# Query and key projections and scores of the last context attention from rounded high parts and remainders

## The reference

```python
x = x + _L3_xattn_ref(_layernorm(x, axis=-1), ctx_1024, ctx_1024, ...)

B, S, D = (1, 1024, 256)
H, DK, DV = (16, 64, 64)
q = (queries @ Wq.T + bq).reshape(b, sq, H, DK).transpose(0, 2, 1, 3)
k = (keys @ Wk.T + bk).reshape(b, sk, H, DK).transpose(0, 2, 1, 3)
v = (values @ Wv.T + bv).reshape(b, sk, H, DV).transpose(0, 2, 1, 3)
scores = jnp.einsum('bhqd,bhkd->bhqk', q, k) / jnp.sqrt(jnp.float32(DK))
causal = jnp.triu(jnp.ones((sq, sk), bool), k=1)
scores = jnp.where(causal, jnp.float32(-jnp.inf), scores)
attn = jax.nn.softmax(scores, axis=-1)
out = jnp.einsum('bhqk,bhkd->bhqd', attn, v)
out = out.transpose(0, 2, 1, 3).reshape(b, sq, H * DV)
return out @ Wo.T + bo
```

## Time and profile before

| | |
|---|---|
| median of three executions | 1660.79 us |
| span of the profiled execution | 1661.7 us |
| TensorE busy | 1562.1 us, 94% of the span |
| VectorE, ScalarE, GpSimd busy | 66%, 55%, 28% |
| share of TensorE in the chain that ended last | 72% |
| TensorE busy in 1380 to 1570 us, in the stage `l3_xattn` | 189.2 of 190 us |
| VectorE, ScalarE, GpSimd busy there | 109.3, 104.4, 59.7 us |
| mean granted clock of TensorE | 0.987 |

### The profile page before, as it was taken

One profiled execution on the slowest core, in us unless ns is written; L12 is line 12 of the kernel. 1 busy time (PEld: TensorE's weight loads), 2 busy tenths in 40 slices (PEclk: granted clock), 3 DMA queues, 4 the chain that ended last, 5 costly groups with the idle time before them and its releaser, 6 DMA issues.

```text
span 1661.7 us, 22981 instructions
## 1 busy us (share of the span) xinstructions
PE 1562.1 (94%) x7755; PEld 844.1 (51%) x7755; DVE 1089.4 (66%) x2220; ACT 908.5 (55%) x1750; POOL 466.0 (28%) x565
## 2 busy tenths in 40 slices
PE   8999999989998999999979999999988989999998
PEld 3476454448784444444335555555344445545446
DVE  7764054775547799999658888887367526555515
ACT  5432233534336677778557777877325635555613
POOL 0220100120000555555205655656020103323300
PEclk9999999999999999999999999999998999999999
DMA  6001000010010000000254311110166020000000
GB/s 244 1 1 27 19 0 1 38 76 1 26 31 15 10 20 10 11 10 30 82 184 147 105 30 30 44 44 21 45 161 166 25 83 24 13 22 12 1 1 26
DMA packets 37707, 76.25 MB, mean 46 GB/s; under 512 B 4507, under 2 KB 23451, under 8 KB 36155
## 3 DMA queue, kind: packets, MB, share of 16 engines
q1 hardware_dynamic: 37590, 74.78, 14.0%
HBM read 57.89 MB, written 16.78 MB: 45 GB/s over the span
## 4 chain that ended last, share of the span: by engine, by line
PE 72%; DVE 12%; issue 7%; ACT 6%; SPq 1%; POOL 1%; PEldq 1%; DMA 1%; PEld 0%; DVEq 0%; POOLq 0%; ACTq 0%
PE ps L2499 6%; PE ps L2081 3%; PE ps L3418 3%; PE ps L2057 3%; PE ps L2103 3%; PE ps L2488 3%; PE ps L3383 3%; PE ps L3393 3%; PE ps L3438 2%; PE ps L230 2%; PE ps L2510 2%; PE ps L2067 2%; PE ps L3411 2%; PE ps L3451 2%; PE ps L857 2%
## 5 line engine op out<-in xcount | busy, mean ns | idle before, releaser
L2754 POOL TENSOR_TENSOR work<-work,arena_b 128x512 f32<-128x512 f32 x128 | 168.4, 1318 | 115.9 <-ACT work L2618 115.9
L2708 DVE CUSTOM_DVE_ANT_0 work<-ps,arena_a 128x1024 f32<-128x1024 f32 x128 | 154.6, 1209 | 0.4 <-PE ps L2488 0.4
L2600 ACT ACTIVATE work<-work,small 128x1024 f32<-128x1024 f32 x128 | 146.8, 1147 | 4.3 <-DVE small L2708 4.3
L2499 PE MATMUL ps<-identity,work 128*128 128x128 f32 x1024 | 139.0, 277 | 6.0 <-ACT work L2618 1.8
L2499 PEld LDWEIGHTS ps<-identity,work 128*128 128x128 f32 x1024 | 115.1, 142 | 54.6 <-issue 29.4
L3600 POOL TENSOR_SCALAR ctx_keys<-ctx_keys,small 128x128 f32<-128x128 f32 (+3 forms) x128 | 66.9, 535 | 173.3 <-DVE small L3525 173.3
L2720 DVE TENSOR_TENSOR work<-ps,arena_b 128x512 f32<-128x512 f32 x128 | 87.9, 686 | 32.9 <-PE ps L2499 30.8
L2618 ACT ACTIVATE work<-ps 128x512 f32<-128x512 f32 x128 | 76.3, 596 | 57.9 <-PE ps L2499 55.0
L2273 POOL TENSOR_SCALAR work<-work 128x1024 f32<-128x1024 int32 x64 | 66.6, 1040 | 100.7 <-DVE work L2228 100.3
L2488 PE MATMUL ps<-work 96*128 96x512 bf16 x256 | 79.3, 393 | 13.5 <-DVE small L2708 7.7
L3477 ACT ACTIVATE ctx_keys<-ctx_keys,small 128x128 f32<-128x128 f32 (+3 forms) x128 | 70.7, 553 | 28.6 <-DVE small L3517 28.0
(11 more groups left out here) (454 smaller groups left out, 3532.8 us busy)
## 6 DMA issues: line engine op xcount, KB each, us to landing
work<-parts_k_L_xattn SPq DMA_DIRECT2D x14, 384.0 KB, 3.9
arena_a<-in_mask SPq DMA_DIRECT2D x2, 2048.0 KB, 7.5
arena_b<-in_groupT SPq DMA_DIRECT2D x2, 2048.0 KB, 9.7
head_weights<-in_w_L_xattn SPq DMA_DIRECT2D x8, 449.0 KB, 3.3
arena_a<-in_w_l_attn SPq DMA_DIRECT2D x1, 3072.0 KB, 16.1
head_weights<-in_w_L_attn SPq DMA_DIRECT2D x8, 384.0 KB, 3.1
work<-parts_q_L_attn SPq DMA_DIRECT2D x8, 384.0 KB, 4.5
work<-parts_k_L_attn SPq DMA_DIRECT2D x8, 384.0 KB, 5.2
```

The lines of the kernel that those rows point to most:

```text
L2499: mm = pe.transpose(t_psum[z][:, kt * P:(kt + 1) * P], prob[i % NP][:, o:o + P], k.iden[:, :])
L2600: act.activation(p, p, ACT.Exp, scale=-1.0, bias=minmax[:, i % 8:i % 8 + 1], accum_out=sums[:, i % 8:i % 8 + 1]).then_inc(*exped.up())
L2708: dve.tensor_tensor_reduce(prob[i % NP], s_psum[i % NS], NEG[:, b, qt, :], -1.0, BIG * 3e8, OP.add, OP.min, minmax[:, i % 8:i % 8 + 1]).th ...
L2754: pool.tensor_tensor(p, p, GT[:, b, 4:8, qt * P:(qt + 1) * P], OP.mult).then_inc(*weighed_pool.up())
```

## The change

Queries, keys and their inputs are each held as a rounded high part and the exact remainder, and each product of two such numbers becomes three: high by high, high by low, low by high. The lowest product is left out.

- Normalisation: VectorE writes the rounded high part of each block, then the full one as before, then the remainder (`Norm.scale`), for both halves.
- Context: GpSimd splits it once, in the stage before; weights: GpSimd splits those of each group, two groups ahead, at the end of the group before (`CausalParts`).
- Chunks of q and k: six matmuls for two. ScalarE reads the bank first and writes the rounded high part, with bias; VectorE reads it again and writes the remainder, and only then is the bank free. The chunks of v stay as they are.
- Scores: six matmuls for two. The factor 0.125 moves into the maximum instruction.
- q and k of one batch of a group lie in rings of three buffers of 512 columns, for two of 1024.
- The weight rounding of the following stage uses one scratch piece for four.

```diff
     def scale(self, dve, n):
         k, dst = self.k, self.dst[n]
         dve.wait_ge(*self.rooted(n + 1))
+        if self.high:
+            for c in range(DC):
+                dve.tensor_tensor(self.high[n][c], dst[:, c, :], self.tmp[n], OP.mult).then_inc(*self.topped.up())
         for c in range(DC):
             final = dst[:, c, :] if self.put is None else self.put[n][:, c, :]
             if self.w is None:
@@ -252,6 +265,12 @@
             dve.wait_ge(*self.scaled(2 * n + c + 1))
             op = dve.tensor_scalar(final, dst[:, c, :], k.col(self.w, c), k.col(self.b, c), OP.mult, OP.add)
         op.then_inc(*self.out.up())
+        if self.high:
+            dve.wait_ge(*self.topped(2 * n + 2))
+            dve.wait_ge(*self.out(n + 1))
+            for c in range(DC):
+                dve.tensor_tensor(self.low[n][c], dst[:, c, :], self.high[n][c].bitcast(F32),
+                                  OP.subtract).then_inc(*self.rest.up())
...
+        if nxt:
+            causal_parts.split_context(pool)
...
+        if nxt:
+            causal_parts.split_weights(pool, 0, k.ahead["l3_xattn"][0](1))
...
+    def split_context(self, pool):
+        for n in range(B):
+            for c in range(DC):
+                pool.tensor_scalar(self.ctx_high[n][c], self.raw[n][c], 1.0, 0.0, OP.mult, OP.add).then_inc(*self.ctx_top.up())
+        for x in range(B * DC - 1):
+            self.split_low(pool, x)
+
+    def split_low(self, pool, x):
+        n, c = divmod(x, DC)
+        pool.wait_ge(*self.ctx_top(x + 1))
+        pool.tensor_tensor(self.ctx_low[n][c], self.raw[n][c], self.ctx_high[n][c].bitcast(F32),
+                           OP.subtract).then_inc(*self.ctx_rest.up())
+
+    def split_weights(self, pool, g, loaded):
+        pool.wait_ge(*loaded)
+        for j in range(2):
+            pool.tensor_scalar(self.w_high[g % 2][j], self.w_raw[g % 2][j], 1.0, 0.0, OP.mult, OP.add).then_inc(*self.w_top.up())
+        for j in range(2):
+            pool.wait_ge(*self.w_top(2 * g + j + 1))
+            pool.tensor_tensor(self.w_low[g % 2][j], self.w_raw[g % 2][j], self.w_high[g % 2][j].bitcast(F32),
+                               OP.subtract).then_inc(*self.w_rest.up())
...
-    q = [view(w, s * K, NT) for s in range(2)]
-    kT = [view(w, (2 + s) * K, NT) for s in range(2)]
+    parts = k.ahead["causal_parts"]
+    blocks = k.rounded("causal_qk", "work", 0, 4 * K)
+    q_high, k_high, q_low = ([view(blocks, (3 * o + j) * S, S) for j in range(min(3, 8 - 3 * o))] for o in range(3))
+    unused = [k.rounded(f"causal_qk_{c}{n}", "ctx_feat", c * NT * 2 + n * S2 + S, S)[:, :] for c in range(DC) for n in range(B)]
+    q_low, k_low = [*q_low, unused[0]], unused[1:]
+    qk_high, qk_low = dict(q=q_high, k=k_high), dict(q=q_low, k=k_low)
...
+    QK = [x for x, ch in enumerate(CHUNKS) if ch[1] != "v"]
+    place = {CHUNKS[x][:3]: y + 1 for y, x in enumerate(QK)}
+    made = lambda g, n: max(place[g, "q", n], place[g, "k", n])
...
-    chunk_out = lambda x: {"q": q_out, "k": k_out, "v": v_out}[CHUNKS[x][1]](2 * CHUNKS[x][0] + CHUNKS[x][2] + 1)
+    chunk_out = lambda x: (v_out(2 * CHUNKS[x][0] + CHUNKS[x][2] + 1) if CHUNKS[x][1] == "v" else rest(place[CHUNKS[x][:3]]))
...
-                n, q0 = n_keys(i), b * S + qt * P
+                n = n_keys(i)
+                j = (2 * g + b) % 3
                 if i % nk == 0:
-                    pe.wait_ge(*q_out(2 * g + b + 1))
-                    pe.wait_ge(*k_out(2 * g + b + 1))
+                    pe.wait_ge(*rest(made(g, b)))
                 if i >= 2:
                     pe.wait_ge(*maxed(2 * i - 2))
-                for h in range(nh):
-                    r = slice(h * rows, (h + 1) * rows)
-                    mm = pe.matmul(s_bank[i % 2][:, h, 0:n], q[g % 2][r, q0:q0 + P], kT[g % 2][r, b * S:b * S + n],
-                                   start=True, stop=True)
+                for qs, ks in ((q_high, k_high), (q_high, k_low), (q_low, k_high)):
+                    for h in range(nh):
+                        r = slice(h * rows, (h + 1) * rows)
+                        mm = pe.matmul(s_bank[i % 2][:, h, 0:n], qs[j][r, qt * P:(qt + 1) * P], ks[j][r, 0:n],
+                                       start=ks is k_high and qs is q_high, stop=qs is q_low)
...
-                    src, t0 = (k.Hn, n * S) if what == "q" else (k.ctxT, n * S2)
+                    high, low = (parts.x_high, parts.x_low) if what == "q" else (parts.ctx_high, parts.ctx_low)
+                    w_high, w_low = (ws[g % 2][what == "k"] for ws in (parts.w_high, parts.w_low))
+                    pe.wait_ge(*parts.w_rest(2 * g + 2))
                     for c in range(DC):
-                        if g == 0 and what == "q":
-                            pe.wait_ge(*ln.rows(n, c))
-                        mm = pe.matmul(ps, W[g % 2][what == "k"][:, c, :], src[:, c, t0:t0 + S], start=c == 0,
-                                       stop=c == 1)
+                        if g == 0:
+                            pe.wait_ge(*(ln.topped if what == "q" else parts.ctx_top)(2 * n + c + 1))
+                        pe.matmul(ps, w_high[:, c, :], high[n][c], start=c == 0, stop=False)
+                        pe.matmul(ps, w_low[:, c, :], high[n][c], start=False, stop=False)
+                    for c in range(DC):
+                        if g == 0:
+                            pe.wait_ge(*(ln.rest if what == "q" else parts.ctx_rest)(2 * n + c + 1))
+                        mm = pe.matmul(ps, w_high[:, c, :], low[n][c], start=False, stop=c == 1)
...
-                if what == "k":
+                if what != "v":
+                    y = 2 * g + n
                     act.wait_ge(*part(x + 1))
-                    if g >= 2:
-                        act.wait_ge(*scored(per * (g - 1)))
-                    act.activation(kT[g % 2][:, half(n)], chunk_bank(x), ACT.Identity,
-                                   bias=weights[g % 2][:, 897:898]).then_inc(*k_out.up())
+                    if y >= 3:
+                        act.wait_ge(*scored(nk * (y - 2)))
+                    act.activation(qk_high[what][y % 3], chunk_bank(x), ACT.Identity,
+                                   bias=weights[g % 2][:, 896 + (what == "k"):897 + (what == "k")]).then_inc(*top.up())
...
-                    dve.tensor_tensor_reduce(prob[i % NP][:, h, 0:n], s_bank[i % 2][:, h, 0:n], causal[:, S - n:S], -1.0,
+                    dve.tensor_tensor_reduce(prob[i % NP][:, h, 0:n], s_bank[i % 2][:, h, 0:n], causal[:, S - n:S], -0.125,
...
-                if what == "q":
-                    dve.wait_ge(*part(x + 1))
-                    if g >= 2:
-                        dve.wait_ge(*scored(per * (g - 1)))
-                    dve.tensor_scalar(q[s][:, half(n)], chunk_bank(x), weights[s][:, 896:897], 0.125, OP.add,
-                                      OP.mult).then_inc(*q_out.up())
+                if what != "v":
+                    y = (2 * g + n) % 3
+                    dve.wait_ge(*top(place[g, what, n]))
+                    dve.scalar_tensor_tensor(out=qk_low[what][y], in0=chunk_bank(x),
+                                             scalar=weights[s][:, 896 + (what == "k"):897 + (what == "k")],
+                                             in1=qk_high[what][y].bitcast(F32), op0=OP.add, op1=OP.subtract).then_inc(*rest.up())
...
+        parts.split_low(pool, B * DC - 1)
+        pool.wait_ge(*ln.var_done(2))
+        parts.split_weights(pool, 1, w_in[1](1))
...
+            if step % per == per - 1 and step // per + 2 < G:
+                g = step // per + 2
+                parts.split_weights(pool, g, w_in[g % 2](g // 2 + 1))
```

44 lines of the change are left out of this document (37 added, 7 removed).

## The result

| | before | changed |
|---|---|---|
| median, us | 1660.68 (1659.28 to 1661.01, 4 executions) | 1680.54 (1677.61 to 1686.22, 4 executions) |
| ratio | | 1.0118, 95% interval 1.0103 to 1.0133 |
| profiled execution: time, span | span 1661.7 | 1681.16, span 1679.9 |

The change makes the kernel 1.2% slower; 1674 was forecast, in a range of 1661 to 1685.

The account below looks back on a forecast made before the run. TensorE was taken as the bound in the stage's groups. Start 4.8, groups 1 to 6 5.1, last group -0.4 and clock 3.5 gave +13.0 us on the 1660.8 median: 1674 us, own range 1668 to 1680, wider 1661 to 1685.

Parts of the forecast that it names:

- TensorE's saving, 1.82 per group: TensorE in each group: q and k chunks save 1.28 us, scores 0.54; 1.14 in all at the upper bound.
- The wait of 2.22 before the k chunk: Behind a group's first q chunk, TensorE waits 2.22 us for ScalarE's high part, then VectorE's remainder.
- The wait of 0.3 before the second q chunk: In a group, read-out needs 3.94 us against TensorE's 3.63, so TensorE waits 0.3.
- 0.85 per group: Net loss taken for each of groups 1 to 6, between +0.7 and +1.1 us; +5.1 in all.
- Last group: The last group has no q or k chunks, so it was to change by -0.4 us.
- The start, 4.8: At the stage's start, VectorE's added scaling work delays TensorE's second q chunk by 4.8 us.
- hidden: GpSimd's splits of context and weights were taken to cost 0, with up to 3.5 us as bound for the weights.
- The clock, 3.5: One fall of TensorE's clock at the start and one in the groups: 3.5 us, bounds 0 and 13.6.
- a fall in every wait: Rival: TensorE's clock falls in all eight waits, 8 x 1.7 = 13.6 us, giving 1684 us; chance 0.12.
- open weight loads: Rival: score products pay for their weight loads each time, +8.5 us over 8 groups, 1682 us; chance 0.09.
- Both heads run side by side: Assumed for scores; the rival had rounded operands run one head after the other, 1692 us; chance 0.04.
- Faster: Rival: TensorE stays the bound in the groups; whole faster if the k chunk's wait is under about 1.1 us; 1654; chance 0.13.

Follow-up runs that it names:

- chunks alone: Changed kernel with q and k read out once in full precision and full-precision scores; chunks still three rounded products, start as changed: 1659.8 us.
- whole change with both mends: Changed kernel with ScalarE's order altered where it reads out a group's first q chunk (high part, exps, copy), plus the rearranged normalisation start: 1656.1 us.
- high-part-first run: Changed kernel with ScalarE's order high part, exps, copy of the value product, only where it reads out a group's first q chunk: 1664.5 us.
- GpSimd late: Changed kernel with GpSimd's last context remainder and its split of group 1's weights behind later signals at the start: 1672.8 us.
- matmuls in the wait: Changed kernel with nine bfloat16 matmuls, results unused, on TensorE inside the wait before the k chunk: 1675.3 us.
- three kernels with the same start: Copy behind the high part, high part first and matmuls in the wait, all with the changed kernel's start: 41.6, 41.6 and 41.9 us in start and group 0.
- scores alone: Changed kernel with chunks as two full-precision products, nothing split beforehand, start as before; two-step read-out and three-product scores kept: 1683.0 us.
- new start: Changed kernel with ScalarE writing the input's high parts, VectorE centring the second half earlier and delaying its remainders, GpSimd's last context remainder later: 1672.4 us.
- copy behind the high part: Changed kernel with ScalarE's copy of the value product moved behind the exps and the chunk's high part in every step: 1682.8 us.

## Why the prediction was right, and where it was not

The direction and the mechanism held; the median is 6.5 us above the forecast, just above its own range and inside the wider one. Term by term, by the table above (changed less before, 21.6 us in the stage; the rest of the kernel differs by 3.4 us the other way between the two profiled executions, with 34 us at 0.50 outside the stage instead of 44):

- *TensorE's saving, 1.82 per group.* Right. Chunks 1.28 (chunks alone, 27.46 to 26.18). A chunk is 1.58 from start to start, not 1.49; what comes before it is 0.08 shorter, so the sum holds. Scores 5.93 to 5.40 us in a group, 0.53, forecast 0.54: 0.89, 0.72, 0.55 and 0.48 for 512 to 128 keys, forecast 0.90, 0.73, 0.56 and 0.5; the first 128 keys of a group take 0.60. From 512 to 256 columns the time falls in proportion, 0.17 us per 128 keys; at that slope 128 keys would take 0.38, so here the proportion ends, as the forecast's 0.5 allowed for. (The 0.62 in the expectation of the whole change with both mends is too much.)
- *The wait of 2.22 before the k chunk.* Right: 2.2 as the forecast counts it, 2.03 of idle time in the rows. The wait of 0.3 before the second q chunk is 0.25. Group 0 has 0.54 us where the forecast had 2.22. The chain is the one named; the high-part-first run, where only ScalarE's order differs, shows it.
- *0.85 per group.* 4.0 us over six groups once the clock is held up, 0.66 each. The forecast's own sum was 0.7; it was raised to 0.85 for a dearer pair of 128 keys that didn't come. Last group -0.6, forecast -0.4: there the scores save 0.5 and the rest is not read.
- *The start, 4.8.* Right for what it counts: the kernel with GpSimd late loses 5.5 in the start and group 0, of which 0.6 is the lowered stretch on its variance (2.50 us from its start to ScalarE's instruction behind it, before 1.92), so 4.9. But the term took VectorE's instructions at the durations of the earlier trace rows, with nothing beside them. GpSimd's work at that place was counted as hidden, since TensorE doesn't wait for it; it was not free, as it stretched VectorE's instruction beside it: 1.10 us in the first half and 0.54 in the second, 1.6 in all.
- *The clock, 3.5.* This is the term that failed. Forecast: two falls in all of 1.7. Found: the clock at 0.50 for 13.65 us in the start and group 0, and in four stretches in the groups. In the groups that is 6.5 us, by the kernel with matmuls in the wait; at the start 4.7 by difference to the kernel with GpSimd late, and the 0.6 that this still has: 11.8 together, of which some 2 at the start are of the profiled execution, as three kernels with the same start show. The upper bound, a fall in every wait, was the better guess for the size: with the scores alone just that happened, in the changed kernel it was four groups of six. The argument against it, that TensorE is dense on both sides of each wait, was refuted: TensorE is dense there too, and the earlier trace rows already showed a gap of 2.08 us with a fall behind it.

With these the sum is 4.9 + 1.6 for the start, 4.0 for the groups, -0.6 for the last, 11.8 for the clock = 21.7, against 21.6 measured in the stage. That it closes is no proof, since the 4.7 is itself a difference between two of the stretches.

The rivals: open weight loads are out, since a pair of 512-key scores with six loads took 0.89 us, and the six products of a chunk, each with a load for the full array, follow each other at 0.23 us. By the sentence of the Trainium skill that I had cited there (TensorE: Matmul & The Clock Gate, Part 3, The mechanism), that a load overlaps with running matmuls only where the row group differs, the loads would have stood open, and the trace disagrees. The same section also lets a load go ahead into a background weight buffer; these rows fit that. Both heads run side by side: their six products of 512 columns take 0.89 us, the six of a chunk 1.58.

"Faster" was right for the groups and wrong for the whole. With the high part first TensorE waits 0.7 us in a group, under the 1.1 of its condition, and the groups are 6.8 us faster than before; but the kernel is still 0.2% slower, since the start and group 0 cost 9.5 us and not 4.8, with the clock and GpSimd in them. Only with the new start too is it faster.

## What to carry to other kernels

A tensor that is now read out in two steps on two engines puts the first engine's whole queue ahead of the second step; look at what stands there, and put the first step ahead of work that is not yet wanted, at that place only. An idle time of 2 us on a dense TensorE is to be priced with a fall of its clock in every repetition, as an upper bound: it came behind three to six of six such waits here, at 1.1 to 1.8 us each. Work on GpSimd that nobody waits for still has a price where VectorE works from SBUF beside it.

## What was not expected of the hardware

- VectorE's tensor_tensor of 128x512, both operands in SBUF, takes 0.60 us of its queue, and 1.70 where GpSimd's tensor_tensor of 128x512 (1.41 us, 1.26 alone) runs beside it: 2.39 for the two. With the two apart both rows fall to the usual. The Trainium skill (GPSIMD Engine Reference, 1. Specifications) says that GpSimd shares its SBUF interfaces with VectorE and contends with VectorE instructions that have two SBUF inputs; these rows agree, and the forecast didn't use it. In the changed kernel's second half GpSimd's 128x256 took 1.18 instead of 0.74 us and VectorE's pair 1.83 instead of 1.29.
- Waits of 2.03 us on a dense TensorE were followed by a granted clock of 0.50 in four of six groups of the changed kernel and of the one with GpSimd late, in three of six with the new start, and waits of 2.07 with longer work behind them in six of six with the scores alone. With waits of 1.0 and 1.5 us in each group (the copy behind the high part) it fell in one group of seven, the last, whose two waits of 1.5 us are 10 us apart. With nine matmuls in the wait it fell in none. What decides it in between stays open.
